# Memory attention in another order: logarithm, totals, and gaps ahead of pair products and query transposes

## The reference

```python
q = _ln((x @ Wq.T + bq).reshape(-1, 48, 16), gq, bq_ln)       # 48 heads of 16
scores = einsum('bnd,nkd->bnk', q, key)                         # 64 keys a head
sc = softmax over the 8 largest of each 64 scores, 0 elsewhere
out = (einsum('bnk,nkd->bnd', sc, value) + q @ Wres.T + bres) @ Wmem.T + bmem
head_k, head_v, head_q = thirds of out                          # 16 heads of 64 each
hq, hk = elu(head_q) + 1, elu(head_k) + 1
lo = causal linear attention of hq, hk, hv, divided by its sum
return _ln(h + lo @ Wo.T, g_out, b_out)
```

## Time and profile before

| What | us |
|---|---|
| Median of 3 runs | 4503.36 (4493.08 to 4503.57) |
| The profiled execution | 4485.82 |
| Its span | 4484.5 |
| Memory attention | about 768 of it |
| DVE busy in 100 to 700 us | 477.27 |
| PE busy in 100 to 700 us | 526.15 |
| ACT and POOL busy in 100 to 700 us | 364.34 and 390.87 |

### The profile page before, as it was taken

How to read it: one execution, slowest core, us unless ns; L and a number is a source line. 1 busy time by engine, 2 the same in 40 slices (tenths; PEclk the granted TensorE clock), 3 DMA queues, 4 the chain that set the end, 5 groups by cost and what they waited for, 6 DMA issues and landing times. The chain is left out here.

```text
span 4484.5 us, 52962 instructions
## 1 busy us (share of the span) xinstructions
PE 3254.5 (73%) x17693; PEld 2099.2 (47%) x17693; DVE 2467.1 (55%) x6511; ACT 1627.5 (36%) x3647; POOL 1403.0 (31%) x1086
## 2 busy tenths in 40 slices
PE   5988886868906666666888888467689567667698
PEld 3666665646602222223566656245456323235455
DVE  6878774364337788885323323545442277765443
ACT  3666653111205444542333333324212244434311
POOL 3666664104352434452212211200010244430010
PEclk7888888879958889898999999679769788889889
DMA  2000001203440000000000000110111200000000
GB/s 88 5 8 8 6 8 39 92 19 102 115 137 0 0 0 0 0 0 14 7 1 1 1 1 1 37 77 1 65 51 28 71 0 0 0 26 1 1 1 19
DMA packets 71034, 116.12 MB, mean 26 GB/s; under 512 B 28689, under 2 KB 58537, under 8 KB 68018
## 3 DMA queue, kind: packets, MB, share of 16 engines
q1 hardware_dynamic: 61170, 86.50, 5.7%
q0 software_dynamic: 9600, 26.23, 2.3%
HBM read 88.58 MB, written 24.12 MB: 25 GB/s over the span
## 5 line engine op out<-in xcount | busy, mean ns | idle before, releaser
L1223 POOL TENSOR_TENSOR L_attn_state<-L_attn_state,L_attn_ccol 128x1024 f32<-128x1024 f32 x192 | 451.7, 2353 | 589.3 <-DVE L_attn_state L1216 586.6
L1216 DVE TENSOR_TENSOR_SCAN L_attn_state<-L_attn_decay,bank 128x1024 f32<-128x1024 f32 x192 | 438.3, 2283 | 25.0 <-PE bank L1182 10.4
L1182 PE MATMUL bank<-L_attn_state,ident 128*128 128x512 f32 x768 | 408.1, 661 | 28.6 <-POOL L_attn_state L1223 28.6
L1176 PE MATMUL bank<-L_attn_parts,L_attn_select 96*128 96x512 bf16 x384 | 133.7, 432 | 257.5 <-DVE bank L1208 246.1
L1193 ACT ACTIVATE L_attn_decay<-L_attn_dt,L_attn_A 128x512 f32<-128x512 f32 x384 | 256.1, 715 | 142.9 <-DVE L_attn_state L1216 139.5
L1102 POOL TENSOR_TENSOR L_xattn_prob<-L_xattn_prob,L_xattn_inv 128x1024 f32<-128x1024 f32 x64 | 121.1, 1893 | 567.0 <-DVE L_xattn_inv L1085 567.0
L1208 DVE TENSOR_TENSOR bank<-L_attn_dtx,bank 128x1024 f32<-128x1024 f32 x192 | 235.9, 1229 | 72.2 <-PE bank L1176 66.4
L1182 PEld LDWEIGHTS bank<-L_attn_state,ident 128*128 128x128 f32 x768 | 161.2, 212 | 190.9 <-issue 122.8
L1198 ACT COPY L_attn_ccol<-bank 128x512 f32<-128x512 f32 x192 | 111.9, 583 | 309.3 <-PE bank L1176 186.8
L1176 PEld LDWEIGHTS bank<-L_attn_parts,L_attn_select 96*128 96x128 bf16 x384 | 28.8, 103 | 396.4 <-DVE bank L1208 355.8
L735 ACT ACTIVATE L_xattn_prob<-bank,L_xattn_top 128x128 f32<-128x128 f32 x512 | 135.4, 415 | 195.6 <-DVE L_xattn_top L777 195.6
(11 more groups left out here) (599 smaller groups left out, 7667.7 us busy)
## 6 DMA issues: line engine op xcount, KB each, us to landing
L_ffn_ew<-in_L_ffn_experts SPq DMA_DIRECT2D x4, 3072.0 KB, 21.1
L_ffn_made<-L_ffn_yout SPq DMA_DIRECT2D x24, 512.0 KB, 3.0
L_ffn_w<-in_L_ffn_w SPq DMA_DIRECT2D x4, 2048.0 KB, 14.7
L_xattn_ctx<-in_ctx_rows SPq DMA_DIRECT2D x3, 2048.0 KB, 8.5
L_ffn_rows<-L_ffn_xh SPq DMA_DIRECT2D x8, 512.0 KB, 2.9
L_ffn_made<-L_ffn_yout SPq DMA_DIRECT2D x12, 256.0 KB, 2.1
L_attn_rows<-in_x SPq DMA_DIRECT2D x16, 128.0 KB, 7.1
turned<-L_attn_rows SPq DMA_DIRECT2D x16, 128.0 KB, 2.3
```

The costliest lines, as they stand in the source:

```text
L1176: pe.matmul(self.spread.bank(2 * N + i)[:, :], self.select[:, NSTATE * i + n, :], parts[:, :], start=True, stop=True).then_inc(*self.sprea ...
L1182: t = pe.matmul(self.y[unit % len(self.y)][m][:, :], self.c.ident[:, :], self.state[N % 3][:, m, :], start=n == 0, stop=n == 15)
L1216: dve.tensor_tensor_scan(flat(self.state[N % 3]), flat(self.decay[N % 2]), flat(self.drive), 0.0, ALU.mult, ALU.add).then_inc(*self.scanne ...
L1223: pool.tensor_tensor(state[:, :, :], state[:, :, :], self.ccol[N % 2][:, :].unsqueeze(1).broadcast_to([P, 2, GT]), ALU.mult).then_inc(*sel ...
```

## The change

It moves steps in the list; every instruction, tile and buffer stays. Three edits:

- "log" n-1 now stands ahead of "exp" n-2.
- "total" n now stands ahead of "spare" n, where it was the last step of the iteration.
- Steps named "rest", which no engine knows, take up slots: one in `front`, ahead of the first query transposes, and three at the head of `attend`.

By the last edit `attend` is one iteration later throughout (pair products in r5, masked copies in r5 and r0, the mixes in r0 and r1, output product and "y" in r2, "ynorm" and "store" in r3), and the query transposes and copies are one slot later: first transposes in slot 1 of r4, their copy in slot 2, second transposes in slot 3, second copy at the head of r5.

```diff
         def front(a):
             return [...
-                    ("scale", a), ("qmul", a), ("qturn", 2 * a), ("qcopy", 2 * a), ("qturn", 2 * a + 1), ("qcopy", 2 * a + 1)]
+                    ("scale", a), ("qmul", a), ("rest", a), ("qturn", 2 * a), ("qcopy", 2 * a), ("qturn", 2 * a + 1), ("qcopy", 2 * a + 1)]
 
         def attend(a):
-            return [("pair", 2 * a), ("sm", 2 * a), ...
+            return [("rest", a)] * 3 + [("pair", 2 * a), ("sm", 2 * a), ...
...
+            if 0 <= n - 1 < UNITS:
+                yield "log", n - 1
             if 0 <= n - 2 < UNITS:
                 yield "exp", n - 2
-            if 0 <= n - 1 < UNITS:
-                yield "log", n - 1
...
             if n < UNITS:
+                yield "total", n
                 yield "spare", n
...
             if 0 <= n - 4 < UNITS:
                 yield "recall", n - 4
-            if n < UNITS:
-                yield "total", n
```

More of the change, by code:

```diff
@@ L2386, in front @@
             return [("norm", a), ("xturn", a), ("xcopy", a), ("query", 2 * a), ("qadd", 2 * a), ("query", 2 * a + 1), ("qadd", 2 * a + 1), ("square", a), ("qsum", a),
-                    ("scale", a), ("qmul", a), ("qturn", 2 * a), ("qcopy", 2 * a), ("qturn", 2 * a + 1), ("qcopy", 2 * a + 1)]
+                    ("scale", a), ("qmul", a), ("rest", a), ("qturn", 2 * a), ("qcopy", 2 * a), ("qturn", 2 * a + 1), ("qcopy", 2 * a + 1)]
         def attend(a):
-            return [("pair", 2 * a), ("sm", 2 * a), ("pair", 2 * a + 1), ("sm", 2 * a + 1), ("mix", 2 * a), ("den", 2 * a), ("oT", 2 * a), ("mix", 2 * a + 1), ("den", 2 * a + 1),
+            return [("rest", a)] * 3 + [("pair", 2 * a), ("sm", 2 * a), ("pair", 2 * a + 1), ("sm", 2 * a + 1), ("mix", 2 * a), ("den", 2 * a), ("oT", 2 * a), ("mix", 2 * a + 1), ("den", 2 * a + 1),
                     ("oT", 2 * a + 1), ("out", a), ("y", a), ("ynorm", a), ("store", a)]
```

## The result

The changed kernel takes 4508.04 us (median of 20 runs, 4501.60 to 4514.81), the kernel before 4501.09 (20 runs, 4493.08 to 4505.68): a ratio of 1.0015, 95% interval 1.0009 to 1.0021. That is inside the 0.3% that counts as no change, but it is a loss of 7 us where a gain of 3 was forecast. The profiled execution took 4501.6 us with a span of 4500.3; that of before took 4485.82, less than any of its 20 runs, so the two spans differ by 15.8 us where the medians differ by 7.

A forecast was written before the change was run, and what follows sets the result against it. No engine was the bound alone; a 43.09 us row cycle was. Legs 17.5 + 25.5 = 43.0, taken as 42.9: 0.2 us in 14 rows, 3 us, so 4483 profiled, 4500 us median; range 4456 to 4526, likeliest 4490 to 4515.

The forecast's parts named there:

- likeliest case: Whole kernel: gains and losses nearly balance, median 4500 us, within 4490 to 4515; chance 0.40.
- leg 5: From sm through replacements, maxima and sm again (5.6 us) and xh (0.40) to the next xturn, at 25.5.
- leg 1: PE from xturn through r0, r1 and r2 to the end of the output product: 17.5 us.
- Leg 2: Output product end through "y", qsum, scaling, maxima and base of r3 to the end of qmul: 6.2 us.
- Leg 3: r3's shift waits for qmul, then exp, rcopy, ACT's small steps and first query copy: from 6.2 to 12.0 us.
- rival D: POOL's shift gets in ahead of qmul; exp and all behind it 0.94 us earlier: 13 us, 4487; chance 0.08.
- Leg 4: PE waits 4.6 us at the second transposes, then transposes, recall, score and pair product at half speed: 7.4 us.
- Sum: One row's cycle, all legs added: 17.5 + 25.5 = 43.0 us, taken as 42.9, against 43.1 before.
- rival B: PE's half clock reaches second pair product and r5's recall and score: 2 us a row slower, 4528; chance 0.14.
- the wait of sm: Sign: the DVE's wait for the pair product, 4.6 us a row, falls to 4 or less, now in r5.
- The logarithm "at nothing": Logarithm ahead of exp: removes the DVE's 1.8 us a row wait; exp's wait for the total costs ACT nothing.
- rival C: Total without cover in r5 and r0, at most 1.6 us each; half the bound 22 us slower, 4522; chance 0.08.

The follow-up runs named there:

- e5: The changed kernel with qmul of r3 ahead of base and an empty slot in its old place: 4485.21 us, 0.9991 of the kernel before.
- e13: The changed kernel with qsum of r2 ahead of "y": 4474.36 us, 0.9962 of the kernel before.
- e1: The changed kernel with the logarithm back behind exp: 4510.16 us, 1.0027 of the kernel before.
- e10: The kernel before with the gaps ("rest" steps) and nothing else: 4505.77 us, 1.0015 of the kernel before.
- e2: The changed kernel with the total back at the end of the iteration, behind the replacements: 4495.58 us, 0.9996 of the kernel before.
- e6: The changed kernel with the recall of r4 ahead of the second query transposes: 4452.06 us, 0.9916 of the kernel before.
- e12: The changed kernel with r4's recall ahead of the second query transposes and the total back behind the replacements: 4460.44 us, 0.9915 of the kernel before.

## Why the prediction was wrong in its sign

The size was small either way: 4500 was forecast, 4508 came, in the range of 4490 to 4515 of the likeliest case. That is luck in part: the forecast was a difference of two numbers near 43, 42.9 against 43.09, one leg was 2.4 us off, and other legs gave most of it back. The legs one by one, after against forecast:

- **Legs 1 and 5 together**: 22.9 us against 23.5, right. The cut between them was wrong: I had xturn ahead of r0's turn and mixes, and in the list it stands behind them, so 2 us belong to leg 5 (7.6, not 6.0; leg 1 is 15.3, not 17.5). It changes nothing in the sum.
- **Leg 2, the step that failed**: output product end to qmul end, 359.38 to 367.96 = 8.6 us against 6.2. I saw that "y" and qsum stand together, but costed the scaling at 0.3, where it takes 1.29 beside POOL's pick, gave ACT's scale no time, and had qmul first and the shift waiting for it. The DVE comes to base 5.6 us after the product instead of 4.2, but the forecast had base wait for kept until 5.3, and kept does end at 5.2, so only 0.3 us of the longer scaling counts. From the base's start to qmul's start it is 0.5 us, its own 0.15 and a wait of 0.33 for ACT's scale, which ends at 365.39. POOL is free in this half microsecond, the shift gets in ahead, and qmul takes 2.53, not 0.94. 0.3 + 0.5 + 1.6 is the 2.4. e5 shows the order: with qmul ahead of base it takes 0.96, the leg is 7.0 us and the period falls by 0.9. e13 shows what qsum behind "y" costs, together with the order: the scaling is back at 0.19, the leg is 6.1 us and the period falls by 1.4.
- **Leg 3**: 4.9 us against 5.8. The shift, being first, doesn't wait. So this is rival D's event with D's price wrong: D took 0.94 us off, as if the path went from the shift through exp. It goes from qmul through total, replacements (368.01 to 369.64), maxima and differences of r4 to ACT's small exponential at 371.49 and the query copy, and what qmul loses, the path loses. e1 shows it, where exp comes 1 us earlier for nothing. In e5, with the order that I had forecast, this leg is 6.0 us.
- **Leg 4**: 7.5 us against 7.4. The wait before the second transposes is 2.91 in this row (45.3 / 14 = 3.2 in the mean), not 4.6, because PE is held up by 1.48 for qmul and 0.98 for scopy first; what I had as one wait of 4.6 and one of 0.6 are three that sum to 5.4. The half speed behind it is right, but in this row not for my reason, as the clock shows below.
- **Sum**: 15.3 + 8.6 + 4.9 + 7.5 + 7.6 = 43.9, and that row's period is 387.94 - 344.07 = 43.87. Two of twelve rows are longer, 332.78 to 378.35 = 45.6: their second pair product is still at half speed (2.08 us at 336.24 where 1.16 is usual). That is rival B's event, in two rows of twelve, 3.3 us in all, so a quarter of the 12.5 that the twelve rows lost. e1 has it in four rows, e10 in five and e13 in six, each by one trace; what decides in which rows it comes was not tried.

```profile
336.24 2.08 PE L2555 MATMUL bank<-L_attn_fq,L_attn_fk 64*128 64x128 f32 x16 [0.49 <-DVE L_attn_sm L2783]
```

The signs I had named divided like this. Right: the kept wait and base's wait for the logarithm gone, a wait before the second query transposes with ACT's copy as releaser, the clock of 100 to 700 us near 0.86 (0.85). Wrong: the period outside 42.5 to 43.5, the wait of sm not at 4 or less (4.5), the wait for the copy not at 4 to 5 (3.2).

The three edits aren't a sum. The logarithm "at nothing" holds in neither case: it gains 0.12% to 0.19% on top of the gaps and costs 0.38% on the kernel before, and the total ahead of spare costs 0.12% to 0.19% under the gaps (e10 to e1, e2 to the change), 5 to 9 us, less than half of rival C's 22 us and by another way than C's, and nothing with the recall moved. What the total costs under the gaps is in leg 2. With the total last in the iteration (e10, e2), qmul starts 0.8 us ahead of the shift in every row, takes 1.64 us, and the leg is 7.5 and 7.3 us. With the total ahead of spare (e1 and the change), the shift is 0.2 us ahead from the second row on, qmul takes 2.53, and the leg is 8.6. The usual row grows from 43.56 (e10) and 43.32 (e2) to 43.87, 4 to 8 us in 14 rows, and e5, which turns the order back and leaves the total, takes 0.24% off. So the total's move, which I had put at nothing, is what let the shift in ahead of qmul. With the recall moved, the leg is 8.6 us in e6 and 7.3 in e12, and the period is 41.0 in both, so there the difference doesn't count. Why the first rows lose 3 us and the tail gains 6 wasn't tried.

What I overlooked beside the sum is larger than what I looked for. I wrote that the recall, the score and the pair product are queued behind the wait for the query copy, and took the order as given. The recall doesn't need that copy, and moving it (e6) is worth 0.99% against the change; e13's move 0.53%.

## What to carry to other kernels

When a wait moves in an in-order queue, list what stands behind it and ask of each whether it needs what is waited for; here the largest gain of a single move came from a recall of 3.8 us that didn't. Put work that is ready ahead of an instruction that will wait, never behind it (qsum and "y"), and where two engines hold each other up, work out which path each loser is on before giving the order of the two a sign. Here one leg was off by 2.4 us and the sum of 43 by 0.9, so a difference of 0.2 has no sign.

## What the runs showed of the hardware

**In half of the rows the clock fell before the long wait.** Stretches of the changed kernel, and below them of e13: length, busy time of PE, PEld, DVE, ACT and POOL with the numbers of their instructions, and then the granted clock, the third number from the end:

```profile
361.40:364.90 3.50, 3.48 (x25) 2.37 (x24) 3.36 (x12) 1.77 (x5) 2.59 (x3) 1.00 0.00 0
364.90:368.10 3.20, 0.74 (x5) 0.33 (x5) 2.87 (x6) 1.42 (x5) 2.86 (x2) 0.88 0.00 0
368.10:370.10 2.00, 1.94 (x8) 1.54 (x8) 2.00 (x20) 1.98 (x4) 1.84 (x3) 0.50 0.00 0
```

```profile
355.00:356.20 1.20, 1.09 (x10) 0.86 (x8) 1.20 (x15) 0.21 (x1) 1.20 (x1) 1.00 0.00 0
356.20:360.60 4.40, 0.01 (x1) 0.01 (x1) 3.12 (x25) 3.91 (x8) 4.24 (x6) 0.87 0.09 21
360.60:367.80 7.20, 7.20 (x38) 5.61 (x38) 2.72 (x17) 4.36 (x9) 4.84 (x4) 0.50 0.11 27
```

With the change PE is busy for 0.74 of 3.20 us between two short waits (0.98 and 1.48), and from 368.10 on the clock is 0.50, the 1.2 GHz level, before the wait of 2.91. The first query transposes take 1.09 us here and in six more of the 14 rows, 0.63 to 1.01 in the other seven. In e6, without that wait, the recall is as slow. In e13 the first query transposes still run at 1.00 (0.63 us for what takes 1.09 after), and the clock falls in the wait of 4.49. So two short waits with little work between them stood ahead of the fall in this row, and one long wait ahead of the other. The Trainium skill, "TensorE: Matmul & The Clock Gate", section "HAM oscillation — how this bites in real kernels", speaks of single gaps between bursts; the trace agrees for e13, and in this row of the changed kernel no single long gap stands ahead of the fall.

**Small DVE instructions are held up too.** The scaling, a TENSOR_SCALAR of 128x48, took 0.19 us alone (e13), 1.29 beside POOL's pick (the change), and 0.32 in the same row of the kernel before. The Trainium skill, "SBUF — State Buffer", section "Who interferes with whom", says that such an instruction can take the port pair that the DVE shares with GpSimd and that the order of issue decides who blocks; 1.29 against 0.19, and 2.53 for qmul behind the shift against 0.96 ahead of it, agree.
